# A recurrent network of two groups, one phase apart: the encoder's pass cut in two, its second layer in another PSUM bank, and five small operations moved

## The chip, the cores and the metric

The kernel runs on one core of a Trainium2 chip. The metric is the device time of one execution in microseconds (us), as the median of three runs. Engines are named as the profile names them: PE (TensorE's matmuls), PEld (its weight loads), DVE (VectorE), ACT (ScalarE), POOL (GpSimd) and SP (SyncE, which here only starts DMAs).

## The reference

2048 sequences run through 256 steps. Each step needs the state of the step before:

```python
def step(carry, xy):
    xt, yt = xy
    st, err, gs, mem, h1, c1, h2, c2 = carry
    encoded = jnp.tanh(xt @ We + st @ Ue + be)
    new_state = jnp.tanh(jnp.einsum('bd,cds->bcs', xt, Wx) + jnp.einsum('bs,cst->bct', st, Ws) + bk)
    inp = jnp.concatenate([encoded, err[:, None]], axis=1)
    mem = jnp.concatenate([inp[:, None, :], mem[:, :-1, :]], axis=1)
    a = jax.nn.relu(mem.reshape(b, -1) @ enc_w1 + enc_b1)
    agent_in = jax.nn.relu(a @ enc_w2 + enc_b2)
    h1, c1 = _lstm_cell(agent_in, h1, c1, lstm_wih1, lstm_whh1, lstm_b1)
    h2, c2 = _lstm_cell(h1, h2, c2, lstm_wih2, lstm_whh2, lstm_b2)
    gate = jax.nn.softmax(h2 @ gate_w + gate_b, axis=1)
    theta = _clamp01(jnp.mean(jnp.abs(mem[:, :10, -1]), axis=1) * 2.5)[:, None]
    gate = gate * theta + gs * (1.0 - theta)
    st = jnp.einsum('bc,bcs->bs', gate, new_state)
    pred = _clamp01(st[:, -1])
    err = pred - yt
    return ((st, err, gate, mem, h1, c1, h2, c2), pred)
```

Eight candidate states (C = 8) of 32 numbers each are mixed by a gate of 8; the memory holds 20 entries of 25 numbers; the encoder's first layer has 64 outputs, the cells 16.

## The kernel before

The batch is cut into two groups of 1024 sequences. A *round* is one phase of the program: it takes one group one step further, so there are 512 rounds, and the two groups alternate. `phase(items)` is written once for each engine. It works on up to three items, `new`, `cur` and `old` (a group at one step, at three stages of its way), in the order in which the code stands; each engine runs its own list in that order, and semaphores (`q_...`) tie the lists together. So what an engine does next is fixed, and if it waits, everything behind waits with it.

What happens to one item, by line:

- L293 transposes the group's state into PSUM, ACT copies it out (L498), L327 multiplies it for the entry, and ACT takes the tanh (L504) and an fp16 copy (L511). POOL makes the rest of the fp16 pair (L944), which SP writes into the history.
- The encoder's first layer is summed in the PSUM bank `a_ps`: 24 history matmuls (L378), spread over PE's list as filler, and the newest entry (L389). ACT takes its relu in one pass over 512 columns (`encoder1`, L517). The second layer (`encoder2`, L400) is written over the first columns of the same bank, and ACT and DVE each take half of its relu (`agent_input`, L525 and L737).
- Cell 0: ACT lays the bias into `chain` (`bias_of_cell`, L543), PE adds the products (L417, 16 records), ACT takes the tanhs (L550, L555), DVE forms the cell's terms (L705, L711), ACT a tanh (L560), DVE the hidden state (L720). Cell 1 goes the same way (the second L417 of a round, the first L705 and L711 after it), up to L729.
- The gate: logits (L427, L434), their peak (L752) and the difference from it (L757) on DVE, the exponential on ACT (`exponentials`, L574), sum, reciprocal and product on DVE (L763, L768, L774, L781). POOL makes one minus theta (`kept_share`, L877), the kept gate (`kept_gate`, L884), the exponentials times theta (L891) and the gate in SBUF (L899). DVE makes theta (`thetas`, L687) late in its phase, behind L729.
- The mix: DVE multiplies half of the candidates by the gate (L792), POOL the other half in two instructions (L911, 128x512 each; the second one also waits for the tanh of candidates' quarter 0, the L536 behind L525). DVE sums over the candidates in four instructions (`mix_sum`, L810), of which the last two stand behind the hidden state of cell 0 (L720). Their result is the next L293's input.
- POOL also keeps the new error and the prediction (`new_error` L968, `keep_prediction` L977), behind `kept_gate`.

Ahead of the loop DVE splits the candidates' and the gate's biases into fp16 pairs (L637 to L641), then the encoder's weights (L647, L648), then the rest, and sets `s_ready` (L676). SP starts the loads of weights, all five slots of x and y, and, behind `s_ready`, the first three slices of the history's weights (L223). PE waits for `s_ready` and for the bias pairs (`s_fix`).

Of the kernel before, what the change touches and what calls it, by code (L numbers as in the profile page):

```python
# [13 lines left out]
P = 128  # L14
GROUPS = 2
# [26 lines left out]
def recurrent_kernel(nc, x_l, y_l, y, error0, gate0, w, ident_c, columns_c, out):  # L42
    ctx = ExitStack()
    with ctx:
# [6 lines left out]
        def sem(name):  # L51
# [25 lines left out]
        ones = sb("ones", [P, TILES])  # L77

# [47 lines left out]
        s_out, s_ys, s_hist0 = sem("s_out"), sem("s_ys"), sem("s_history_zero")  # L126
        s_x = [sem(f"s_x_slot{u}") for u in range(PER_TILE)]
# [4 lines left out]
        (q_trps, q_st, q_zps, q_enc, q_predps, q_err, q_eh, q_el, q_aps, q_a, q_inps, q_in,  # L132
         q_candps) = (
            sem(f"q_{n}") for n in ("trps", "st", "zps", "enc", "predps", "err", "eh", "el", "aps", "a",
# [14 lines left out]
        q_in_high = sem("q_in_high")  # L149
        q_xh, q_xl = sem("q_xh"), sem("q_xl")  # L150
        q_bias = [sem(f"q_bias{c}") for c in range(2)]
        q_hkept = sem("q_hkept")
        q_sum = [[sem(f"q_sum{hf}_{pair}") for pair in range(2)] for hf in range(HF)]
# [45 lines left out]
        def _(sp):  # L199
# [11 lines left out]
            for t in range(PER_TILE):  # L211
# [4 lines left out]


            sp.wait_ge(s_parts, 1)
            sp.dma_start(gate_bias[1:2, :], gate_bias_low[0:1, :]).then_inc(s_fix, 16)
            sp.dma_start(cand_bias[1:P:D_IN, :], cand_bias_low[0:P:D_IN, :]).then_inc(s_fix, 16)  # L220
# [6 lines left out]
            sp.wait_ge(s_ready, 1)  # L227
            history_weights(w_slot(-1), PER_TILE)
            history_weights(0, PER_TILE + 1)
            history_weights(1, PER_TILE + 2)  # L230

# [53 lines left out]
        def _(pe):  # L285
            pe.wait_ge(s_ready, 1)
            pe.wait_ge(s_fix, 16 * 2)

            def state_transpose(item, hf):
                g, n, u = item  # L290
                for pair in range(2):
                    pe.wait_ge(q_sum[hf][pair], n)
# [41 lines left out]
            def candidates_bias(item):  # L334
                g, n, u = item
                for q in CAND_ORDER:
                    pe.wait_ge(q_cand[q], n)
# [106 lines left out]
            def phase(items, extra):  # L444
# [21 lines left out]
                if cur:  # L466
                    cell_gates(cur, 0)
                    candidates_bias(cur)
                    candidates_x(cur)
                    candidates_s(cur)  # L470
# [9 lines left out]
        def _(act):  # L480
# [11 lines left out]
            act.dma_start(ys[:, :, :], y.rearrange("(n p) t -> p n t", p=P)).then_inc(s_ys, 16)  # L492
            act.wait_ge(s_ready, 1)
# [607 lines left out]
```

## Time and profile before

| | |
|---|---|
| median of 3 runs | 5336.49 us (5336.03 to 5337.18) |
| the profiled execution: its time, its span | 5342.21 us, 5340.3 us |
| granted TensorE clock of that execution | 0.998 |
| busy share of the span | PE 97%, PEld 59%, DVE 84%, ACT 79%, POOL 57% |

The span is the time from the first to the last instruction of the profiled execution. Busy shares are means over the whole span. PE's is high by nature: a matmul's record reaches to the end of its pipeline, and records overlap, so 97% leaves room for waits that no row shows as idle time.

### The profile page before, as it was taken

To read this page: it belongs to the slowest core of one execution; us is meant where nothing else is said; L and a number is where in the kernel's file an instruction comes from. 1 tells how busy PE (TensorE), PEld (TensorE's weight loads), DVE (VectorE), ACT (ScalarE), POOL (GpSimd) and SP (SyncE) were. 2 spreads that over 40 slices of the span, in tenths; PEclk is the share of its full clock that TensorE was granted. 3 is DMA by queue.
4 is the path that set the end of the run, shared out by engine and by line. 5 is a ranking of instruction groups with operands and counts; after the bars stand their busy time and mean duration, and the time that the engine had idled before them with its cause. 6 is when DMAs were issued, how large, how long until landed. Compare 5 with 4: busy or idle time off the path is not lost.

```text
span 5340.3 us, 193942 instructions
## 1 busy us (share of the span) xinstructions
PE 5165.0 (97%) x68608; PEld 3158.5 (59%) x68608; DVE 4468.2 (84%) x11824; ACT 4233.4 (79%) x10241; POOL 3060.8 (57%) x6149
## 2 busy tenths in 40 slices
PE   7999999999999999999999999999999999999998
PEld 4555555555555555555555555555555555555554
DVE  7888888888888888888888888888888888888887
ACT  6887877878888878788787788788877878777886
POOL 4555555555555555555555555555555555555555
PEclk9999999999999999999999999999999999999999
DMA  2111111111111111111111111111111111111111
GB/s 68 31 30 33 30 33 30 33 30 33 30 33 30 31 31 30 33 30 33 30 33 30 33 30 33 30 32 30 30 33 30 33 30 33 30 33 30 33 30 41
DMA packets 299271, 172.29 MB, mean 32 GB/s; under 512 B 156598, under 2 KB 263866, under 8 KB 298698
## 3 DMA queue, kind: packets, MB, share of 16 engines
q1 hardware_dynamic: 293560, 159.45, 11.9%
q8 instruction: 564, 9.24, 0.7%
q10 hardware_dynamic: 5138, 3.53, 0.2%
q14 instruction: 9, 0.07, 0.0%
HBM read 74.55 MB, written 2.10 MB: 14 GB/s over the span
## 4 chain that ended last, share of the span: by engine, by line
PE 94%; ACT 4%; issue 2%; DVE 0%; DMA 0%; POOL 0%; ACTq 0%; POOLq 0%; DVEq 0%
PE a_ps L378 27%; PE chain L417 21%; PE a_ps L389 9%; PE cand_ps L359 8%; PE cand_ps L350 6%; PE chain L327 6%; PE chain L320 4%; ACT state_t L498 4%; PE chain L293 4%; PE a_ps L400 3%; PE cand_ps L340 3%; PE chain L434 1%; PE chain L427 0%; DMA gate_bias_stage<-in_gate_b 0%; DVE enc_table L648 0%
## 5 line engine op out<-in xcount | busy, mean ns | idle before, releaser
L378 PE MATMUL a_ps<-hist,w_hist 125*64 125x512 f16 x12288 | 1816.5, 383 | 25.2 <-DMA w_hist<-enc_table 24.0
L810 DVE TENSOR_REDUCE state<-mixed 128x64 f32<-128x512 f32 x2048 | 1353.4, 682 | 34.2 <-POOL mixed L911 0.8
L911 POOL TENSOR_TENSOR mixed<-cand,gate 128x512 f32<-128x512 f32 x1024 | 1285.3, 1277 | 48.6 <-POOL gate L899 12.5
L417 PEld LDWEIGHTS chain<-cell_in,cell_w 128*64 128x64 f32 x16384 | 903.2, 136 | 488.7 <-ACT cell_in L525 248.5
L417 PE MATMUL chain<-cell_in,cell_w 128*64 128x128 f32 x16384 | 1120.5, 277 | 41.5 <-issue 1.4
L536 ACT ACTIVATE cand<-cand_ps 128x512 f32<-128x512 f32 x2048 | 1107.0, 594 | 13.3 <-issue 0.4
L378 PEld LDWEIGHTS a_ps<-hist,w_hist 125*64 125x64 f16 x12288 | 695.8, 109 | 568.8 <-issue 298.1
L933 POOL CAST x_parts<-x_sb 128x256 f16<-128x256 f32 x512 | 203.8, 398 | 953.2 <-DVE cell_in L720 938.4
L550 ACT ACTIVATE gates<-chain 128x384 f32<-128x384 f32 x1024 | 503.5, 492 | 251.2 <-PE chain L417 251.2
L705 DVE SCALAR_TENSOR_TENSOR added<-gates 128x256 f32<-128x256 f32 x1024 | 620.8, 606 | 57.2 <-ACT gates L550 3.7
L877 POOL TENSOR_TENSOR one_theta<-ones,theta 128x8 f32<-128x8 f32 x512 | 105.3, 206 | 950.0 <-DVE theta L687 950.0
L543 ACT ACTIVATE chain<-cell_bias 128x512 f32<-128x512 f32 x1024 | 611.0, 597 | 16.1
L792 DVE TENSOR_TENSOR mixed<-cand,chain 128x1024 f32<-128x1024 f32 x512 | 616.4, 1204 | 0.2 <-issue 0.2
L560 ACT ACTIVATE tanh_c<-gates 128x128 f32<-128x128 f32 x1024 | 318.8, 311 | 305.1 <-DVE gates L711 305.0
L389 PE MATMUL a_ps<-entry,w_now 100*64 100x256 f32 x4096 | 555.0, 388 | 0.0
L359 PE MATMUL cand_ps<-w_s,state_t 32*128 32x256 f32 x8192 | 529.3, 375 | 0.0
L350 PE MATMUL cand_ps<-w_x_parts,x_parts 32*128 32x256 f16 x12288 | 421.5, 268 | 0.0
L327 PE MATMUL chain<-state_t,w_ue 128*64 128x256 f32 x2048 | 334.1, 405 | 87.4 <-ACT state_t L498 87.1
L517 ACT ACTIVATE a_sb<-a_ps,columns 128x512 f32<-128x512 f32 x512 | 352.3, 688 | 69.6 <-PE a_ps L389 0.8
L359 PEld LDWEIGHTS cand_ps<-w_s,state_t 32*128 32x128 f32 x8192 | 356.5, 186 | 24.7
L938 POOL TENSOR_TENSOR x_parts<-x_sb,x_parts 128x256 f16<-128x256 f32 x512 | 344.6, 673 | 41.1
L350 PEld LDWEIGHTS cand_ps<-w_x_parts,x_parts 32*128 32x128 f16 x12288 | 315.7, 93 | 71.7
(80 smaller groups left out, 7348.5 us busy)
## 6 DMA issues: line engine op xcount, KB each, us to landing
x_sb<-in_x_l SPq DMA_DIRECT2D x260, 256.0 KB, 2.7
hist<-entry_parts SPq DMA_DIRECT2D x2048, 25.0 KB
w_hist<-enc_table SPq DMA_DIRECT2D x258, 128.0 KB, 2.4
y_rows<-in_y_l SPq DMA_DIRECT2D x260, 8.0 KB
ys<-in_y ACTq DMA_DIRECT2D x1, 2048.0 KB, 16.7
preds_out<-preds SPq DMA_DIRECT2D x1, 2048.0 KB, 7.5
cand<-in_encoder ACTq DMA_DIRECT2D x1, 640.0 KB, 3.8
cell_w<-in_cell ACTq DMA_DIRECT2D x2, 256.0 KB, 5.3
```

What stands on the lines that cost most here:

```text
L327: last = nc.tensor.matmul(chain[g][rows, Z_AT:Z_AT + COLS], w_ue[:, rows], state_t[:, g, :], start=False, stop=True, skip_group_check=True)
L350: nc.tensor.matmul(cand_ps[q][:, NS * hf:NS * hf + NS], x_parts[rows, g, xp, P * hf:P * hf + P], w_x_parts[rows, wp, :], start=False, stop ...
L359: last = nc.tensor.matmul(cand_ps[q][:, NS * hf:NS * hf + NS], state_t[rows, g, P * hf:P * hf + P], w_s[rows, :], start=False, stop=True, ...
L378: nc.tensor.matmul(a_ps[g][ENC * half:ENC * half + ENC, :], w_hist[0:HROWS, w_slot(u), kk, wp, :], hist[0:HROWS, xp, k, at:at + 512], star ...
L389: last = nc.tensor.matmul(a_ps[g][rows, COLS * p:COLS * p + COLS], w_now[0:ER, p, rows], entry[0:ER, g, :], start=False, stop=True, skip_g ...
L417: last = nc.tensor.matmul(chain[g][rows, P * r:P * r + P], cell_w[c][:, hf, r, :], cell_in[c][:, g, hf, :], start=False, stop=True, skip_g ...
L536: ins = nc.scalar.activation(cand[:, g, q // 2, :, q % 2, :, :].rearrange("p h s c -> p h (s c)"), cand_ps[q][:, :].rearrange("p (h k) -> ...
L543: nc.scalar.activation(chain[g][:, :].rearrange("p (r b) -> p r b", r=4), cell_bias[:, c, :].rearrange("p (r o) -> p r o", o=1).to_broadca ...
L705: V.scalar_tensor_tensor(added[c][:, g, :, :], gates[c][:, g, 1:3, :], 1.0, gates[c][:, g, 3:5, :], ALU.add, ALU.mult).then_inc(q_added[c], 1)
L792: V.tensor_tensor(mixed[:, 1, :, :, :, :].rearrange("p h l s c -> p (h l) s c"), cand[:, g, 1, :, :, :, :].rearrange("p h l s c -> p (h l) ...
L810: V.tensor_reduce(state[:, g, hf, 2 * pair:2 * pair + 2, :], mixed[:, pair, hf, :, :, :], AX, ALU.add)\
L911: G.tensor_tensor(mixed[:, 0, :, q, :, :], cand[:, g, 0, :, q, :, :], over_s, ALU.mult)\
```

## The change

In the loop: ACT's relu of the first layer becomes two instructions of 256 columns, each with its own semaphore, and the two halves of the second layer's matmuls wait for one each. The second layer's output moves from `a_ps` to `cand_ps[2]`. Cell 0's bias is laid ahead of the exponential instead of behind `encoder1`. DVE's theta moves from behind L729 to ahead of cell 1's terms. The last two sums over the candidates become one instruction. POOL keeps error and prediction ahead of one minus theta instead of behind the kept gate. Ahead of the loop: the bias pairs are made behind `s_ready`, PE waits for them at their first use, the history's weights are fetched as soon as their table is there, four slots of x and y behind them, and ACT runs one tanh of eight columns early.

```diff
@@ (ahead of the loop: SP)
+            load_slot(0)
+            sp.wait_ge(s_tables, 1)
             history_weights(w_slot(-1), PER_TILE)
             history_weights(0, PER_TILE + 1)
             history_weights(1, PER_TILE + 2)
+            for t in range(1, PER_TILE):
+                load_slot(t)
+            sp.wait_ge(s_parts, 1)
...
@@ (PE)
             pe.wait_ge(s_ready, 1)
-            pe.wait_ge(s_fix, 16 * 2)
...
+            def candidates_bias(item, extra):
+                g, n, u = item
+                if extra is None:
+                    pe.wait_ge(s_fix, 16 * 2)
...
             def encoder2(item):
                 g, n, u = item
-                pe.wait_ge(q_a, n)
                 for p in range(2):
+                    pe.wait_ge(q_a[p], n)
                     for hf in range(HF):
                         at = AGENT_ROWS[hf].start + 2 * H * p
-                        last = nc.tensor.matmul(a_ps[g][at:at + 2 * H, 0:P], w_enc2[:, :],
+                        last = nc.tensor.matmul(cand_ps[2][at:at + 2 * H, 0:P], w_enc2[:, :],
...
@@ (ACT)
+            act.wait_ge(s_warm, 1)
+            nc.scalar.activation(warm[:, 1, :], warm[:, 0, :], ACT.Tanh)
             act.wait_ge(s_ready, 1)
...
-                nc.scalar.activation(a_sb[:, g, :], a_ps[g][:, :], ACT.Relu, bias=enc1_bias[:, 0:1])\
-                    .then_inc(q_a, 1)
+                for p in range(2):
+                    at = slice(COLS * p, COLS * p + COLS)
+                    nc.scalar.activation(a_sb[:, g, at], a_ps[g][:, at], ACT.Relu, bias=enc1_bias[:, 0:1])\
+                        .then_inc(q_a[p], 1)
...
-                nc.scalar.activation(cell_in[0][rows, g, hf, :], a_ps[g][rows, 0:P], ACT.Relu,
+                nc.scalar.activation(cell_in[0][rows, g, hf, :], cand_ps[2][rows, 0:P], ACT.Relu,
...
                     entry_high(new)
+                    bias_of_cell(new, 0)
                 if cur:
                     exponentials(cur)
                 if new:
                     encoder1(new)
-                    bias_of_cell(new, 0)
                     agent_input(new, 0)
...
@@ (DVE)
+            def last_sums(item):
+                g, n, u = item
+                dve.wait_ge(q_mul[1], n + GROUPS)
+                for q in range(2):
+                    dve.wait_ge(q_mulpool[q], n + GROUPS)
+                V.tensor_reduce(state[:, g, 1, :, :].rearrange("p (a l) s -> p a (l s)", a=2),
+                                mixed[:, :, 1, :, :, :].rearrange("p a l s c -> p a (l s) c"), AX, ALU.add)\
+                    .then_inc(q_sum[1][0], 1)
...
-                    mix_sum(old, 1, 0)
-                    mix_sum(old, 1, 1)
+                    last_sums(old)
                 if cur:
                     error_sum(cur)
                 if old:
                     prediction(old)
                 if cur:
+                    thetas(cur)
                     cell_terms(cur, 1)
...
                     second_hidden(cur)
-                    thetas(cur)
                     peaks(cur)
...
@@ (POOL)
                     next_hidden(old, cur)
+                    new_error(old, extra)
+                    keep_prediction(old, extra)
                 if cur:
                     kept_share(cur)
                     kept_gate(cur)
-                if old:
-                    new_error(old, extra)
-                    keep_prediction(old, extra)
```

How the instructions stand now shows at two places. On ACT, between the entry's fp16 copy and the tanh of candidates' quarter 0, first before and then now (each row: line, operation, output and inputs, shape, the semaphores it waits for; the changed kernel's lines are numbered some ten higher):

```order
L511 ACTIVATE entry_parts<-entry 100x256 [waits q_enc,q_err]
L574 ACTIVATE expd<-logit 128x64 [waits q_logit]
L517 ACTIVATE a_sb<-a_ps,columns 128x512 [waits q_aps]
L543 ACTIVATE chain<-cell_bias 128x512 [waits q_enc]
L525 ACTIVATE cell_in<-a_ps,columns 64x128 [waits q_inps,q_hnext]
L536 ACTIVATE cand<-cand_ps 128x2x256 [waits q_mulpool0]
```

```order
L519 ACTIVATE entry_parts<-entry 100x256 [waits q_enc,q_err]
L553 ACTIVATE chain<-cell_bias 128x512 [waits q_enc]
L584 ACTIVATE expd<-logit 128x64 [waits q_logit]
L527 ACTIVATE a_sb<-a_ps,columns 128x256 [waits q_aps]
L527 ACTIVATE a_sb<-a_ps,columns 128x256
L535 ACTIVATE cell_in<-cand_ps,columns 64x128 [waits q_inps,q_hnext]
```

The 512-column bias write has moved from behind the relu to ahead of the exponential, and the relu is two instructions, of which the second has no wait of its own. On POOL, between the copy of the hidden states and the gate, before and now:

```order
L921 COPY cell_in<-cell_in 128x256 [waits q_h0,q_hkept,s_ready]
L877 TENSOR_TENSOR one_theta<-ones,theta 128x8 [waits q_theta]
L884 TENSOR_TENSOR kept<-gate,one_theta 128x64 [waits q_keptfrom,q_onetheta]
L968 ISA [waits q_errsum,q_pred]
L968 TENSOR_TENSOR err_ring<-pred_now,ys 128x8
L977 REGISTER_ALU [waits q_pred]
L977 COPY preds<-pred_now 128x8
L944 TENSOR_TENSOR entry_parts<-entry,entry_parts 128x256 [waits q_eh]
L891 TENSOR_TENSOR weighted<-expd,theta 128x64 [waits q_exp]
```

```order
L939 COPY cell_in<-cell_in 128x256 [waits q_h0,q_hkept,s_ready]
L986 ISA [waits q_errsum,q_pred]
L986 TENSOR_TENSOR err_ring<-pred_now,ys 128x8
L995 REGISTER_ALU [waits q_pred]
L995 COPY preds<-pred_now 128x8
L895 TENSOR_TENSOR one_theta<-ones,theta 128x8 [waits q_theta]
L902 TENSOR_TENSOR kept<-gate,one_theta 128x64 [waits q_keptfrom,q_onetheta]
L962 TENSOR_TENSOR entry_parts<-entry,entry_parts 128x256 [waits q_eh]
L909 TENSOR_TENSOR weighted<-expd,theta 128x64 [waits q_exp]
```

The two instructions that wait for the prediction now stand ahead of the two that wait for theta; all four stand ahead of the entry's low half, as before.

## Rows read from the trace of the kernel before

**Rows 1.** Line view of the state's transpose: records, first and last start in us.

```profile
L293 PE MATMUL chain<-ident,state x1024: 272/300/412, 28.8 to 5308.3; 128*128 128x128 f32 x171
```

**Rows 2.** Timeline of one round, PE: start us, us, engine, line, operation, count.

```profile
2694.84 0.44 PE L293 MATMUL chain<-ident,state 128*128 128x128 f32 x2
...
2699.96 1.09 PE L417 MATMUL chain<-cell_in,cell_w 128*64 128x128 f32 x16
...
2703.28 0.60 PE L320 MATMUL chain<-x_sb,w_we 128*64 128x256 f32 x4
2703.93 1.09 PE L417 MATMUL chain<-cell_in,cell_w 128*64 128x128 f32 x16
...
2705.17 0.44 PE L293 MATMUL chain<-ident,state 128*128 128x128 f32 x2
```

**Rows 3.** Timeline of the same round, DVE.

```profile
2695.25 0.42 DVE L705 SCALAR_TENSOR_TENSOR added<-gates 128x256 f32<-128x256 f32 x1
...
2696.55 0.29 DVE L729 SCALAR_TENSOR_TENSOR h_second<-gates,tanh_c 128x128 f32<-128x128 f32 x1
...
2701.62 0.80 DVE L705 SCALAR_TENSOR_TENSOR added<-gates 128x256 f32<-128x256 f32 x1
...
2703.86 1.28 DVE L810 TENSOR_REDUCE state<-mixed 128x64 f32<-128x512 f32 x2
```

**Rows 4.** Timeline of the same round, POOL (in brackets: idle us before, and releaser).

```profile
2697.01 0.20 POOL L877 TENSOR_TENSOR one_theta<-ones,theta 128x8 f32<-128x8 f32 x1 [1.89 <-DVE theta L687]
...
2697.85 0.67 POOL L944 TENSOR_TENSOR entry_parts<-entry,entry_parts 128x256 f16<-128x256 f32 x1
2698.48 0.30 POOL L891 TENSOR_TENSOR weighted<-expd,theta 128x64 f32<-128x64 f32 x1
2699.18 0.36 POOL L899 TENSOR_TENSOR gate<-fresh,kept 128x64 f32<-128x64 f32 x1 [0.41 <-DVE fresh L774]
2699.62 2.51 POOL L911 TENSOR_TENSOR mixed<-cand,gate 128x512 f32<-128x512 f32 x2
```

**Rows 5.** Timeline of the same round, ACT.

```profile
2697.01 0.42 ACT L511 ACTIVATE entry_parts<-entry 100x256 f16<-100x256 f32 x1
2697.80 0.26 ACT L574 ACTIVATE expd<-logit 128x64 f32<-128x64 f32 x1 [0.37 <-DVE logit L757]
2698.19 0.69 ACT L517 ACTIVATE a_sb<-a_ps,columns 128x512 f32<-128x512 f32 x1
2698.77 0.59 ACT L543 ACTIVATE chain<-cell_bias 128x512 f32<-128x512 f32 x1
2699.50 0.36 ACT L525 ACTIVATE cell_in<-a_ps,columns 64x128 f32<-64x128 f32 x1
2699.89 0.60 ACT L536 ACTIVATE cand<-cand_ps 128x512 f32<-128x512 f32 x1
```

**Rows 6.** Timeline of rounds 2 and 3, PE.

```profile
38.71 0.60 PE L320 MATMUL chain<-x_sb,w_we 128*64 128x256 f32 x4
39.15 1.04 PE L417 MATMUL chain<-cell_in,cell_w 128*64 128x128 f32 x16
...
40.34 0.44 PE L293 MATMUL chain<-ident,state 128*128 128x128 f32 x2
...
50.53 0.44 PE L293 MATMUL chain<-ident,state 128*128 128x128 f32 x2
```

**Rows 7.** Timeline of round 2, POOL.

```profile
44.38 0.36 POOL L899 TENSOR_TENSOR gate<-fresh,kept 128x64 f32<-128x64 f32 x1 [0.45 <-DVE fresh L774]
```

**Rows 8.** Timeline ahead of the loop, DVE, SP's queue, PE and ACT.

```profile
5.35 2.60 DVE L637 CAST cand_bias<-cand 128x512 f16<-128x512 f32 x1 [0.79 <-DMA gate_bias_stage<-in_gate_b]
...
21.42 2.12 SPq L223 DMA_DIRECT2D w_hist<-enc_table  x3
...
24.01 3.62 PE L378 MATMUL a_ps<-hist,w_hist 125*64 125x512 f16 x16 [24.01 <-DMA w_hist<-enc_table]
...
29.45 1.28 ACT L498 ACT_TABLE_LOAD   x1 [29.45 <-PE chain L293]
```

More of the change, by code:

```diff
@@ L130, in recurrent_kernel @@
         s_hist = [sem(f"s_hist_group{g}") for g in range(GROUPS)]
[L132 removed]
+        (q_trps, q_st, q_zps, q_enc, q_predps, q_err, q_eh, q_el, q_aps, q_inps, q_in,
          q_candps) = (
[L134 removed]
+            sem(f"q_{n}") for n in ("trps", "st", "zps", "enc", "predps", "err", "eh", "el", "aps",
                                     "inps", "in", "candps"))
@@ L149, in recurrent_kernel @@
         q_in_high = sem("q_in_high")
+        q_a = [sem(f"q_a{p}") for p in range(2)]
         q_xh, q_xl = sem("q_xh"), sem("q_xl")
@@ L152, in recurrent_kernel @@
         q_hkept = sem("q_hkept")
-        q_sum = [[sem(f"q_sum{hf}_{pair}") for pair in range(2)] for hf in range(HF)]
+        q_sum = [[sem(f"q_sum0_{pair}") for pair in range(2)], [sem("q_sum1")]]
         block = ctx.enter_context(nc.Block())
@@ L210, in _, with load_slot @@
                 load(err_ring[:, :, 0:1], error0.rearrange("(n p o) -> p n o", p=P, o=1))
-            for t in range(PER_TILE):
+            def load_slot(t):
                 sp.dma_start(x_sb[:, t, :, :].rearrange("p g b -> p (g b)"), x_l[P * t:P * t + P, :])\
@@ L230, in _ @@
             history_weights(1, PER_TILE + 2)
+            for t in range(1, PER_TILE):
+                load_slot(t)
+            sp.wait_ge(s_parts, 1)
+            sp.dma_start(gate_bias[1:2, :], gate_bias_low[0:1, :]).then_inc(s_fix, 16)
+            sp.dma_start(cand_bias[1:P:D_IN, :], cand_bias_low[0:P:D_IN, :]).then_inc(s_fix, 16)
+            sp.wait_ge(s_ready, 1)
             def turn_start(turn):
@@ L286, in _ @@
             pe.wait_ge(s_ready, 1)
-            pe.wait_ge(s_fix, 16 * 2)
             def state_transpose(item, hf):
                 g, n, u = item
-                for pair in range(2):
-                    pe.wait_ge(q_sum[hf][pair], n)
+                for done in q_sum[hf]:
+                    pe.wait_ge(done, n)
                 last = nc.tensor.matmul(chain[g][:, P * hf:P * hf + P],
@@ L622, in _ @@
                 V.memset(gates[n][:, :, 4, :], 0.0)
-            for hf in range(HF):
-                for pair in range(2):
-                    V.memset(state[:, :, hf, 2 * pair:2 * pair + 2, :], 0.0).then_inc(q_sum[hf][pair], GROUPS)
+            for pair in range(2):
+                V.memset(state[:, :, 0, 2 * pair:2 * pair + 2, :], 0.0).then_inc(q_sum[0][pair], GROUPS)
+            V.memset(state[:, :, 1, :, :], 0.0).then_inc(q_sum[1][0], GROUPS)
             V.memset(scratch[:, :, :], 0.0).then_inc(s_prep, 1)
             dve.wait_ge(s_prep, 1)
-            dve.wait_ge(s_biases, 16 * 2)
             steps = [1]
@@ L676, in _ @@
             V.tensor_copy(scratch[:, 1, :], ones[:, :]).then_inc(s_ready, 1)
+            dve.wait_ge(s_biases, 16 * 2)
+            link(V.tensor_copy(cand_bias[:, :], bk_stage))
+            link(V.tensor_tensor(cand_bias_low[:, :], bk_stage, cand_bias[:, :], ALU.subtract))
+            link(V.tensor_copy(gate_bias[0:1, :], gate_bias_stage[0:1, :]))
+            V.tensor_tensor(gate_bias_low[0:1, :], gate_bias_stage[0:1, :], gate_bias[0:1, :], ALU.subtract)\
+                .then_inc(s_parts, 1)
             def error_sum(item):
@@ L736, in agent_input @@
                 dve.wait_ge(q_inps, n)
-                V.tensor_scalar(cell_in[0][rows, g, hf, :], a_ps[g][rows, 0:P], enc2_bias[rows, 0:1], 0.0,
+                V.tensor_scalar(cell_in[0][rows, g, hf, :], cand_ps[2][rows, 0:P], enc2_bias[rows, 0:1], 0.0,
                                 ALU.add, ALU.max).then_inc(q_in_high, 1)
@@ L815, in prediction @@
                 for hf in range(HF):
-                    for pair in range(2):
-                        dve.wait_ge(q_sum[hf][pair], n + GROUPS)
+                    for done in q_sum[hf]:
+                        dve.wait_ge(done, n + GROUPS)
                 V.tensor_scalar(pred_now[:, g, :].rearrange("p (h q) -> p h q", h=HF), state[:, g, :, :, S - 1],
```

16 lines of the change are left out of this document (5 added, 11 removed).

## The prediction

> **What bounds it now.** The page comes first, and its 97% for PE says little, since matmul records overlap. The line view of L293, the first instruction that a round's state needs, gives the unit of account: 1024 records in 512 rounds, from 28.8 to 5308.3 us, so (5308.3 - 28.8) / 511 = 10.33 us a round [rows 1]. Whatever the change does 512 times is counted per round; the rest of the span is some 29 us ahead and 32 us behind. Then I read the timeline of one round of that length engine by engine, all times taken from its L293 at 2694.84.
>
> PE: cell 0's products (L417) start at 5.12, the x part of the entry (L320) at 8.44, cell 1's L417 at 9.09, the next L293 at 10.33 [rows 2]. Where nothing stops PE, in round 1, L417 follows L320 by 0.44 and L293 follows L417 by 1.19 [rows 6]; here it is 0.65 and 1.24. So PE waits about 0.2 us ahead of cell 1, though no row calls it idle.
>
> What it waits for is cell 0's hidden state, done when DVE goes on to the last two sums, at 9.02. Backwards on DVE stands cell 0's L705, which took 0.80, while the same instruction for cell 1 took 0.42 [rows 3]. It ends at 7.58, 0.29 behind POOL's two L911, which ran from 4.78 to 7.29 [rows 4]: DVE's instruction had started at 6.78, but got through only when POOL let go. Backwards on POOL: L911 follows the gate (4.34), the gate the weighted exponentials (3.64), and those start only as L944 (3.01 to 3.68) ends, though the exponential was there at 3.22 [rows 4, 5]. L944 is late because four small instructions stand ahead of it that begin when theta arrives, at 2.17, after 1.89 us of idle time. Theta stands behind L729 on DVE. So the round is one loop: cell 1, theta, POOL's queue, L911, cell 0's L705, hidden state, cell 1.
>
> Round 2 tests this: it had no old error to keep, POOL reached the gate at 44.38 - 40.34 = 4.04, 0.30 sooner than above, and the round lasted 10.19 [rows 6, 7].
>
> **The change, part by part.** *Theta, and error and prediction on POOL.* The four small instructions run as soon as the prediction is out, in time in which POOL idles, so L944 starts when ACT's fp16 copy is there (2.59 and a handover) instead of at 3.01; the weighted product then waits for the exponential. *Bias ahead of the exponential.* It starts when the copy ends at 2.59, less 0.11 by which two ACT instructions overlap (L543 starts 0.11 before L517 ends), and lasts 0.59, to 3.07; the exponential can start at 2.96 as now or 0.02 later [rows 5]. Bounds 0 and 0.11 (no overlap); 0.02 taken. Together they bring the gate and the first L911 about 0.3 forward, as in round 2, to 4.5. The second L911 also needs candidates' quarter 0, whose tanh (5.05 to 5.65 now) follows `agent_input` on ACT. By the next paragraph it ends at 5.79; with some 0.1 of handover the second L911 (half of 2.51) runs from 5.88 to 7.14, L705 ends 0.29 later at 7.43 instead of 7.58, and cell 1's L417 could start 1.51 behind it, as now: at 8.94.
>
> *The relu in halves.* The same kind of instruction (relu with a bias column) takes 0.69 for 512 columns and 0.36 for 128, so about 0.47 for 256 [rows 5]. With the overlap of 0.11 the second half ends 0.36 + 0.47 = 0.83 after the start, where the whole pass ended after 0.69: **0.14 later**. The start does not move, since all halves wait for the last L389. The first half of L400 can go early, but PE is still busy with history matmuls then, and `agent_input` waits for the second half. Bounds of the delay: 0 (no column can be out sooner) and 0.25 (no overlap: 0.94 - 0.69; L536 behind L525 starts 0.03 after its end, so such pairs exist). `agent_input` and cell 0's L417 move by the same 0.14: from 5.12 to 5.26.
>
> The Trainium skill speaks against this part ("ScalarE: Activation LUTs", section What ACT_TABLE_LOAD costs: about 280 ns fixed for an instruction with a bias operand, 0.833 ns a column, 93 ns of overlap). By that page, as an estimate, a half takes 0.49 and the second ends 0.20 later than the whole pass, and the round below would be 0.06 longer. The trace gives 0.69 for 512 columns where the page gives 0.71.
>
> *The second layer's bank.* Same matmuls, same size of reads; `cand_ps[2]` is free between the error's subtraction and the candidates' bias. 0, with no gain or loss in sight: the two banks' users of before and now stand in the same order.
>
> *One sum for two.* Now 1.28 for both; one start-up less, so between 0 and 0.1 saved. They end at 10.30, just ahead of L293, and with DVE's 0.15 of gain at about 10.1. PE comes later than that (below), so this is worth nothing now.
>
> **The sum for a round.** PE's list becomes the limit: L417 of cell 0 at 5.26; L320 behind it by 3.32 as now, 8.58; L417 of cell 1 behind L320 by 0.44, at 9.02, later than the 8.94 that DVE allows; L293 1.19 later, at 10.21. Two things can still lengthen it. Cell 1's chain starts nearer to the next round's L293 now, and L434 leaves little room behind L729; and POOL's four small instructions now run while DVE makes cell 1's terms (L705 from 0.41, L729 to 2.00), where POOL was idle. I take 0.04 for both (bounds 0 and 0.3, see the rivals; near the lower end because these instructions take 0.2 to 0.3 us each, not 2.51). That makes 10.25, 0.08 less than 10.33: 511 x 0.08 = **41 us**.
>
> **Ahead of the loop.** PE's first matmul waited from 21.42 to 24.01 for weights fetched behind `s_ready`: 2.6 go, since the table is now fetched earlier. The load of ACT's table, 1.28 on the first state's way, goes too. The bias pairs leave DVE's way to `s_ready`: L637 took 2.60 [rows 8], but the next instruction may be held by what held it; bounds 0 and 2.6, 1.3 taken. Sum **5 us**. What is moved behind `s_ready` has until round 1's candidates, some 10 us later.
>
> Total 46 us: the profiled execution, 5342.21 us with a span of 5340.3, would take 5296, and the median, which is 5.7 us below that execution, **5290**.
>
> **Rivals.** *No gain in the rounds.* The halves do not overlap: 0.25 instead of 0.14, and the round is 10.21 + 0.11 = 10.32, or 10.36 with the 0.04. With the 5 us ahead of the loop that is 5336 - 5 - 5 to 5336 - 5 + 15: 5326 to 5346. For it: the pair L525 and L536. Against: L517 and L543, which like the halves cover all partitions.
>
> *Slower: POOL's small instructions hold DVE.* What L911 did to cell 0's L705, the four small instructions (about 0.9 us in a row, from the prediction on) do to cell 1's L705 and what follows it. If DVE gets through only where POOL pauses, cell 1's terms come about 0.3 later; L729, L434, L389 and the relu follow directly, and the round is 10.21 + 0.3 = 10.51: + 0.18 x 511 = 92, less 5, so 5424. It decides from about 0.12 of delay on. For it: the 0.80 against 0.42. Against: the instructions are short, and a held instruction of DVE ends only 0.29 behind the one that held it, so it could pass between two of them. No row shows DVE waiting at the border of two POOL instructions.
>
> The Trainium skill has the rule ("SBUF — State Buffer", section Who interferes with whom: a DVE instruction with two SBUF inputs and a GpSimd instruction that reads SBUF exclude each other, and the one that issues first holds the ports for all of its length). The held L705 agrees (0.80 against 0.42). By that rule DVE would get its turn at each border, which is the lesser delay.
>
> *Faster.* The halves cost nothing, or POOL's small instructions don't meet DVE: L417 of cell 0 at 5.12, cell 1's at 8.88, the round 10.07 at best, 5198; half way to it, 5245.
>
> **Chances.** The forecast (round of 10.20 to 10.29): 0.56. No gain: 0.13. Held by POOL: 0.23. More gain: 0.08. About 0.2% (11 us) is what a measurement of this kernel can tell from no change. Faster by more: 0.64; within: 0.13; slower: 0.23. The forecast's own range is 5265 to 5315; to leave out no more than 2 in 10 it goes up into the case of the held DVE, to 5365, and down to 5258.
>
> **What would show it.** Right: two relu records of about 0.47 us, the second ending 0.83 behind the first's start; weighted exponentials right behind the exponential, cell 0's L705 ending by 7.45; L417 of cell 1 following L320 by 0.44; rounds of 10.25; the first L293 some 4 us earlier, and no table load behind it. Wrong: cell 1's L705 or L711 longer than now, and L434 waiting for L729 (the slower rival); the second relu starting at the first's end (no gain); cell 1's L417 still waiting for the hidden state (POOL's queue remained the limit).

## The result, and the profile after

The changed kernel took 5268.01 us (median of 4 runs, 5267.09 to 5268.63), beside 5336.77 (5336.03 to 5337.18) of the kernel before: a ratio of 0.9871, 95% interval 0.9854 to 0.9888. It is faster by 69 us; I had forecast 5290, or 46 to 47 less than before. In the profiled execution the span is 5266.3 us, and the granted clock 0.998, as before. The views below say where the 69 us are.

The line view of the state's transpose, now L297 (records, ns min/median/max, first and last start), answers to [rows 1]:

```profile
L297 PE MATMUL chain<-ident,state x1024: 272/300/381, 24.8 to 5232.6; 128*128 128x128 f32 x171
```

A round is now (5232.6 - 24.8) / 511 = 10.19 us instead of 10.33: 511 x 0.14 = 72 us. The loop begins at 24.8 instead of 28.8, 4 us sooner. What lies behind the last transpose is 33.7 us (5266.3 - 5232.6) instead of 32.0; over the kernels of this study that tail lies between 32.0 and 37.6, so a difference of 2 us there says nothing about the change.

The timeline of one round, PE (start us, us, engine, line, operation, count), answers to [rows 2]; times in the text are taken from its L297 at 2695.04:

```profile
2695.04 0.44 PE L297 MATMUL chain<-ident,state 128*128 128x128 f32 x2
...
2700.26 1.09 PE L423 MATMUL chain<-cell_in,cell_w 128*64 128x128 f32 x16
...
2703.58 0.60 PE L324 MATMUL chain<-x_sb,w_we 128*64 128x256 f32 x4
...
2704.02 1.06 PE L423 MATMUL chain<-cell_in,cell_w 128*64 128x128 f32 x16
...
2705.23 0.44 PE L297 MATMUL chain<-ident,state 128*128 128x128 f32 x2
```

Cell 0's products start at 5.22, 0.10 later than before; cell 1's at 8.98, 0.11 sooner. Between L324 and cell 1's L423 lie 0.44 us instead of 0.65: PE no longer waits for cell 0's hidden state there. In every tenth round POOL's queue still counts: the first L929 starts at 4.68 instead of 4.52, DVE's last sum ends 0.05 later (medians), and the round lasts 10.23 (mean) instead of 10.19.

POOL in the same round (in brackets: idle us before, and releaser) answers to [rows 4]:

```profile
2695.66 0.29 POOL L986 TENSOR_TENSOR err_ring<-pred_now,ys 128x8 f32 x1 [0.34 <-DVE pred_now L837]
...
2695.90 0.19 POOL L995 COPY preds<-pred_now 128x8 f32 x1
...
2696.05 0.29 POOL L895 TENSOR_TENSOR one_theta<-ones,theta 128x8 f32<-128x8 f32 x1
...
2696.42 0.29 POOL L902 TENSOR_TENSOR kept<-gate,one_theta 128x64 f32<-128x64 f32 x1
...
2697.71 0.67 POOL L962 TENSOR_TENSOR entry_parts<-entry,entry_parts 128x256 f16<-128x256 f32 x1 [0.99 <-ACT entry_parts L519]
...
2698.37 0.29 POOL L909 TENSOR_TENSOR weighted<-expd,theta 128x64 f32<-128x64 f32 x1
...
2699.12 0.36 POOL L917 TENSOR_TENSOR gate<-fresh,kept 128x64 f32<-128x64 f32 x1 [0.45 <-DVE fresh L784]
...
2699.56 2.63 POOL L929 TENSOR_TENSOR mixed<-cand,gate 128x512 f32<-128x512 f32 x2
```

The four small instructions are done at 1.67, where the first of them used to start at 2.17. POOL then idles for 0.99 us until ACT's fp16 copy is there, and the entry's low half starts at 2.67 instead of 3.01. The gate follows at 4.08 (4.34), the two L929 end at 7.15 (7.29). The row of the two L929 is longer than before (2.63 against 2.51), since the second waits for a tanh on ACT (L546 below, done at 5.74).

ACT in the same round, answering to [rows 5]:

```profile
2697.21 0.42 ACT L519 ACTIVATE entry_parts<-entry 100x256 f16<-100x256 f32 x1
...
2697.53 0.58 ACT L553 ACTIVATE chain<-cell_bias 128x512 f32<-128x512 f32 x1
...
2698.05 0.24 ACT L584 ACTIVATE expd<-logit 128x64 f32<-128x64 f32 x1
...
2698.39 0.84 ACT L527 ACTIVATE a_sb<-a_ps,columns 128x256 f32<-128x256 f32 x2
...
2699.80 0.36 ACT L535 ACTIVATE cell_in<-cand_ps,columns 64x128 f32<-64x128 f32 x1 [0.57 <-PE cand_ps L406]
...
2700.18 0.60 ACT L546 ACTIVATE cand<-cand_ps 128x512 f32<-128x512 f32 x1
```

The relu in two halves takes 0.84 where one pass took 0.69, and `agent_input` (L535) starts at 4.76 instead of 4.66. That is where cell 0's 0.10 comes from. The exponential starts at 3.01 instead of 2.96.

DVE, answering to [rows 3]:

```profile
2695.45 0.43 DVE L715 SCALAR_TENSOR_TENSOR added<-gates 128x256 f32<-128x256 f32 x1
...
2695.98 0.29 DVE L721 SCALAR_TENSOR_TENSOR gates<-added 128x128 f32<-128x128 f32 x1
...
2696.76 0.29 DVE L739 SCALAR_TENSOR_TENSOR h_second<-gates,tanh_c 128x128 f32<-128x128 f32 x1
...
2701.92 0.55 DVE L715 SCALAR_TENSOR_TENSOR added<-gates 128x256 f32<-128x256 f32 x1
...
2703.92 1.22 DVE L828 TENSOR_REDUCE state<-mixed 128x128 f32<-128x1024 f32 x1
```

Cell 0's L715 is still held by POOL's L929 (0.55, where cell 1's takes 0.43), but ends at 7.43 instead of 7.58. Cell 1's L715 and L721 take what they took before, beside POOL's small instructions. The one last sum (L828) takes 1.22 where the two took 1.28.

Ahead of the loop, answering to [rows 8]: the timeline of POOL, DVE, ACT and PE.

```profile
0.74 6.92 POOL L888 MEMSET hist<- 128x8192 f32 x1 [0.29 <-POOLq L1088]
...
4.66 3.68 DVE L650 CAST enc_table<-cand 128x1280 f16<-128x1280 f32 x1
...
9.90 0.83 DVE L650 CAST enc_table<-cand 128x1280 f16<-128x1280 f32 x1
...
10.07 1.28 ACT L500 ACT_TABLE_LOAD   x1 [10.07 <-issue]
...
19.99 3.62 PE L384 MATMUL a_ps<-hist,w_hist 125*64 125x512 f16 x16 [19.99 <-DVE scratch L679]
```

PE starts 4.0 us sooner and now waits for DVE instead of a DMA. ACT's table is loaded long before its first use. The first L650 is slow because POOL's memset of the history (L888, to 7.66) holds it: it ended at 8.34 or 8.35 in all nine kernels with this edit, though it started anywhere from 4.66 to 4.98. In the two without it, L637 ended at 7.95 and 7.94, 0.28 behind the same memset, from starts at 5.35 and 5.81. No run moved the memset.

### The profile page after: what moved, and what is told of

Its sections match the earlier page's. It is cut to its first block, busy times and chain, and to the rows that moved or that the text cites. A ratio compares the mean times of both kernels' runs of the same rounds, so it can differ in the third digit from the quotient of the medians.

```text
span 5266.3 us, 192919 instructions
## 1 busy us (share of the span) xinstructions
PE 5127.9 (97%) x68608; PEld 3212.5 (61%) x68608; DVE 4347.6 (83%) x11313; ACT 4309.1 (82%) x10754; POOL 3224.3 (61%) x6149
## 4 chain that ended last, share of the span: by engine, by line
PE 94%; ACT 4%; issue 1%; DVE 0%; POOL 0%; POOLq 0%; DVEq 0%; ACTq 0%
PE a_ps L384 28%; PE chain L423 19%; PE a_ps L395 9%; PE cand_ps L365 8%; PE cand_ps L356 6%; PE chain L331 6%; PE cand_ps L406 5%; PE chain L324 4%; ACT state_t L506 4%; PE chain L297 4%; PE cand_ps L346 3%; PE chain L440 1%; PE chain L433 0%; DVE enc_table L650 0%; DVE enc_table L651 0%
## 5 line engine op out<-in xcount | busy, mean ns | idle before, releaser
L929 POOL TENSOR_TENSOR mixed<-cand,gate 128x512 f32<-128x512 f32 x1024 | 1301.9, 1274 | 82.2 <-POOL gate L917 12.5
L546 ACT ACTIVATE cand<-cand_ps 128x512 f32<-128x512 f32 x2048 | 1112.5, 598 | 81.1 <-issue 0.3
L423 PEld LDWEIGHTS chain<-cell_in,cell_w 128*64 128x64 f32 x16384 | 903.3, 136 | 357.4 <-ACT cell_in L535 237.8
L423 PE MATMUL chain<-cell_in,cell_w 128*64 128x128 f32 x16384 | 1105.0, 276 | 7.2 <-issue 0.8
L820 DVE TENSOR_REDUCE state<-mixed 128x64 f32<-128x512 f32 x1024 | 698.9, 682 | 18.6 <-POOL mixed L929 0.8
L962 POOL TENSOR_TENSOR entry_parts<-entry,entry_parts 128x256 f16<-128x256 f32 x512 | 343.9, 672 | 528.8 <-ACT entry_parts L519 528.8
L828 DVE TENSOR_REDUCE state<-mixed 128x128 f32<-128x1024 f32 x512 | 624.7, 1220 | 16.7 <-issue 0.9
L395 PE MATMUL a_ps<-entry,w_now 100*64 100x256 f32 x4096 | 555.3, 388 | 0.0
L715 DVE SCALAR_TENSOR_TENSOR added<-gates 128x256 f32<-128x256 f32 x1024 | 501.1, 489 | 21.4 <-ACT gates L560 4.0
L527 ACT ACTIVATE a_sb<-a_ps,columns 128x256 f32<-128x256 f32 x1024 | 429.1, 470 | 47.6 <-PE a_ps L395 0.3
L535 ACT ACTIVATE cell_in<-cand_ps,columns 64x128 f32<-64x128 f32 x512 | 185.4, 362 | 293.1 <-PE cand_ps L406 293.1
L747 DVE TENSOR_SCALAR cell_in<-cand_ps,columns 64x128 f32<-64x128 f32 x512 | 175.4, 343 | 259.5 <-PE cand_ps L406 259.5
```

The costliest lines, as they stand in the source:

```text
L395: last = nc.tensor.matmul(a_ps[g][rows, COLS * p:COLS * p + COLS], w_now[0:ER, p, rows], entry[0:ER, g, :], start=False, stop=True, skip_g ...
L423: last = nc.tensor.matmul(chain[g][rows, P * r:P * r + P], cell_w[c][:, hf, r, :], cell_in[c][:, g, hf, :], start=False, stop=True, skip_g ...
L546: ins = nc.scalar.activation(cand[:, g, q // 2, :, q % 2, :, :].rearrange("p h s c -> p h (s c)"), cand_ps[q][:, :].rearrange("p (h k) -> ...
L820: V.tensor_reduce(state[:, g, hf, 2 * pair:2 * pair + 2, :], mixed[:, pair, hf, :, :, :], AX, ALU.add)\
L828: V.tensor_reduce(state[:, g, 1, :, :].rearrange("p (a l) s -> p a (l s)", a=2), mixed[:, :, 1, :, :, :].rearrange("p a l s c -> p a (l s) ...
L929: G.tensor_tensor(mixed[:, 0, :, q, :, :], cand[:, g, 0, :, q, :, :], over_s, ALU.mult)\
```

## The experiments

The theory after the result: the round was a loop through POOL's queue; theta and POOL's order took it apart; what limits now is PE's list, behind a relu that its halves made 0.10 us later. The rivals: the halves, their bank, the bias's place or the head brought the gain. The first four kernels undo or keep one part each.

**The relu in one pass again** (all other edits stay; both halves of the second layer's matmuls wait for the one semaphore, which the cut does not show; lines are two lower from the relu on):

```diff
-                for p in range(2):
-                    at = slice(COLS * p, COLS * p + COLS)
-                    nc.scalar.activation(a_sb[:, g, at], a_ps[g][:, at], ACT.Relu, bias=enc1_bias[:, 0:1])\
-                        .then_inc(q_a[p], 1)
+                nc.scalar.activation(a_sb[:, g, :], a_ps[g][:, :], ACT.Relu, bias=enc1_bias[:, 0:1])\
+                    .then_inc(q_a[0], 1)
```

> The changed kernel with the relu of the first layer in one pass of 512 columns again; the second layer keeps its bank cand_ps[2], all other edits stay. My theory: the gain came from theta and POOL's order, the halves only cost 0.10 us a round (the second half ends 0.84 us behind the start of the first, the whole pass 0.69), and PE's list is the limit, so all of it comes back: cell 0's L423 at 5.11 instead of 5.21, rounds of 10.09 instead of 10.19, 511 x 0.10 = 51 us less than the changed kernel: 5217 us (5207 to 5235). Rival one: the second layer's first matmuls, which may start behind half one, are part of the gain: then the time rises above 5268, by up to 51. Rival two: DVE's hidden state, not PE's list, sets the round: then the delay of agent_input is hidden and the time stays within 10 us of 5268.

5222.87 us (5221.38 to 5223.34), ratio 0.9785 (0.9768 to 0.9801): 45 us less than the changed kernel. Its timeline of one round, ACT and PE:

```profile
2702.86 0.44 PE L297 MATMUL chain<-ident,state 128*128 128x128 f32 x2
...
2706.21 0.69 ACT L525 ACTIVATE a_sb<-a_ps,columns 128x512 f32<-128x512 f32 x1
...
2707.52 0.36 ACT L533 ACTIVATE cell_in<-cand_ps,columns 64x128 f32<-64x128 f32 x1 [0.62 <-PE cand_ps L406]
...
2707.98 1.09 PE L423 MATMUL chain<-cell_in,cell_w 128*64 128x128 f32 x16
...
2711.30 0.60 PE L324 MATMUL chain<-x_sb,w_we 128*64 128x256 f32 x4
...
2711.74 1.06 PE L423 MATMUL chain<-cell_in,cell_w 128*64 128x128 f32 x16
...
2712.95 0.44 PE L297 MATMUL chain<-ident,state 128*128 128x128 f32 x2
```

`agent_input` at 4.66, cell 0 at 5.12, cell 1 at 8.88, the next transpose at 10.09: the whole list moved by 0.10. So the halves are the one part of the change that costs, and they cost because PE's list is now the limit. The mean round is (5188.6 - 24.8) / 511 = 10.105, not 10.09, since one round in ten lasts some 10.24 in this kernel, hardly other than the 10.23 that it lasted in the changed one: there POOL's queue still sets the round, not PE's list.

**Theta and POOL's order alone**, in the kernel before:

```diff
                 if cur:
+                    thetas(cur)
                     cell_terms(cur, 1)
...
                     second_hidden(cur)
-                    thetas(cur)
...
                     next_hidden(old, cur)
+                    new_error(old, extra)
+                    keep_prediction(old, extra)
...
                     kept_gate(cur)
-                if old:
-                    new_error(old, extra)
-                    keep_prediction(old, extra)
```

> The kernel before with two edits alone: theta ahead of cell 1's terms on DVE, and error and prediction ahead of one minus theta on POOL. My theory: these two carry the whole gain of the rounds; with the relu in one pass, L417 of cell 0 stays at 5.12, PE's list then gives 8.88 for cell 1 and rounds of 10.08 to 10.12 instead of 10.33: 5337 - 511 x 0.21 to 0.25 = 5209 to 5230 us, faster than the changed kernel. Rival one: the halves, their bank or the bias ahead of the exponential carry it: then the time stays within 15 us of 5337. Rival two: the last two sums in two instructions (1.28 us against 1.22) end too late for the next L293: rounds of about 10.18, 5260 us.

5224.87 us (5224.31 to 5226.96), ratio 0.9788 (0.9772 to 0.9805); rounds of (5189.5 - 28.5) / 511 = 10.10. Three small instructions moved bring 112 us, more than the whole change. The rivals fall.

No run moves theta alone, or error and prediction alone, and round 2 of the kernel before says that the latter may be enough. POOL had no error and prediction to keep there, while theta came as late as ever:

```profile
42.45 0.21 POOL L877 TENSOR_TENSOR one_theta<-ones,theta 128x8 f32<-128x8 f32 x1 [2.41 <-DVE theta L687]
...
43.01 0.67 POOL L944 TENSOR_TENSOR entry_parts<-entry,entry_parts 128x256 f16<-128x256 f32 x1
```

Even so the entry's low half started at 43.01 - 40.34 = 2.67 and the gate at 4.04 [rows 7], which are the medians of the run with theta and POOL's order, and the round lasted 10.19, as long as round 2 of that run. Which of the two moves was needed stays open.

**Everything but theta and POOL's order**, the changed kernel with the diff just shown turned round:

> The changed kernel with theta behind L729's counterpart and with POOL's order as before; halves, bank, bias, one sum and the edits ahead of the loop stay. My theory: POOL's queue is the loop again (theta, the fp16 rest of the entry, weighted exponentials, gate, products, DVE's held cell-0 terms), rounds of 10.30 to 10.35, and only the 5 us ahead of the loop remain of the gain: 5320 to 5345 us. Rival one: the other edits carry the gain: the time stays within 15 us of 5268. Rival two: they carry a part of it: something between, about 5300.

5334.66 us (5333.75 to 5337.82), ratio 0.9996 (0.9986 to 1.0006); rounds of (5299.2 - 24.8) / 511 = 10.32. Its timeline shows the old loop again:

```profile
2698.25 0.44 PE L297 MATMUL chain<-ident,state 128*128 128x128 f32 x2
...
2700.34 0.21 POOL L895 TENSOR_TENSOR one_theta<-ones,theta 128x8 f32<-128x8 f32 x1 [1.81 <-DVE theta L697]
...
2701.18 0.67 POOL L962 TENSOR_TENSOR entry_parts<-entry,entry_parts 128x256 f16<-128x256 f32 x1
...
2701.26 0.24 ACT L584 ACTIVATE expd<-logit 128x64 f32<-128x64 f32 x1
...
2701.81 0.29 POOL L909 TENSOR_TENSOR weighted<-expd,theta 128x64 f32<-128x64 f32 x1
...
2702.97 2.50 POOL L929 TENSOR_TENSOR mixed<-cand,gate 128x512 f32<-128x512 f32 x2
...
2705.13 0.62 DVE L715 SCALAR_TENSOR_TENSOR added<-gates 128x256 f32<-128x256 f32 x1
```

POOL waits 1.81 us for theta, the exponential (done at 3.25) waits for the entry's low half, the two L929 follow each other without a pause. Here the halves of the relu cost nothing: the round is no longer than before the change, though `agent_input` is as late as in the changed kernel (4.76, median). A delay off the limiting loop is free, and the same delay on it cost 45 us.

**The bias behind the relu again**, in the changed kernel:

```diff
                     entry_high(new)
-                    bias_of_cell(new, 0)
...
                     encoder1(new)
+                    bias_of_cell(new, 0)
                     agent_input(new, 0)
```

> The changed kernel with cell 0's bias behind the relu again. My theory: the exponential starts 0.05 us sooner, which nothing waits for now, and the bias write of 0.59 us runs from about 4.1 to 4.7 in ACT's wait for the second layer, which lasts to 4.76: no change beyond 0.02 us a round, 5258 to 5278 us. Rival one: the second half's end and the bias together reach past 4.76, agent_input comes up to 0.10 later: up to 5320 us. Rival two: the 0.05 us of the exponential count, since the gate's chain sets the round: 5243 us.

5268.71 us (5267.89 to 5271.84), ratio 0.987 (0.9854 to 0.9887): the same as the changed kernel, as my theory had it.

**The relu in one pass and the bias behind it**, the first and the last of these diffs together:

> The changed kernel with the relu in one pass and cell 0's bias behind it again: what is left of the change is theta, POOL's order, the one last sum and the edits ahead of the loop. My theory: with the relu whole, the gate's chain and PE's list meet, so the exponential's 0.05 us now count in part: in the run with the relu alone put back, POOL's first L927 ended at 5.80, later than the second could have started (5.74), against 5.76 in the run with theta alone. Rounds of 10.097 instead of 10.105, 4 us less: 5219 us (5214 to 5223), faster than every kernel so far. Rival: the bias's place is free here too, and the time stays at 5223 within 3 us.

5219.59 us (5218.35 to 5220.1), ratio 0.9779 (0.9766 to 0.9793); rounds of (5184.4 - 23.9) / 511 = 10.099. As expected, though the 3 us to the kernel with the relu alone are less than the intervals of the two ratios; only the mean round (10.099 and 10.105) speaks for them. Most of that lies in the tenth rounds, which last 10.19 here and 10.23 there: POOL's queue sets them, and the 0.05 of the exponential counts. Against the run with theta alone it is 5 us, the part ahead of the loop. So one sum for two and the other bank are worth nothing that shows.

**The edits ahead of the loop alone**, in the kernel before:

```diff
+            sp.wait_ge(s_tables, 1)
             history_weights(w_slot(-1), PER_TILE)
...
-            pe.wait_ge(s_fix, 16 * 2)
...
+            nc.scalar.activation(warm[:, 1, :], warm[:, 0, :], ACT.Tanh)
             act.wait_ge(s_ready, 1)
...
-            link(V.tensor_copy(cand_bias[:, :], bk_stage))
...
             V.tensor_copy(scratch[:, 1, :], ones[:, :]).then_inc(s_ready, 1)
+            dve.wait_ge(s_biases, 16 * 2)
+            link(V.tensor_copy(cand_bias[:, :], bk_stage))
...
```

> The kernel before with the edits ahead of the loop alone (history's weights fetched as soon as their table is there, bias pairs behind s_ready, one early tanh). My theory: 4.0 us at the first L293 and 1.2 us in round 1, where the table load stood: 5337 - 5 = 5332 us (5329 to 5335). Rival: the rounds that follow, which are not periodic at first, give it back, or the output's DMA at the end moves as much: 5337 within 2 us.

5332.36 us (5331.97 to 5337.16), ratio 0.9991 (0.9982 to 1.0). The size is as expected, and the trace has the first transpose at 24.8, but the interval reaches to no change.

**What limits next.** In the kernel with the relu in one pass and the bias behind it, the two history matmuls ahead of the transpose are moved behind it:

```diff
-                    history(cur, 2, 2, 3)
                     state_transpose(cur, 0)
                     state_transpose(cur, 1)
                     prediction_transpose(cur)
+                    history(cur, 2, 2, 3)
```

> The kernel of e5_best with the last two history matmuls of PE's phase (0.21 us between cell 1's products and the next state's transpose) moved behind the prediction's transpose, where PE waits 0.39 us for the copy of the state. The transpose can then start 0.21 sooner. If PE's way from cell 1's products to the next transpose sets the round, as my prediction had it, the round falls by up to 0.17 (DVE's last sum then ends last): 5219 - 87 = 5132 us, 5130 to 5180. Rival, which I hold likelier after the first runs: the loop goes from cell 1's products past the transpose, over the tanhs, DVE's L739 and the logits (2.08), which stand in PE's list ahead of the newest entry's matmuls (2.23); the transpose's chain has slack, and the time stays at 5219 within 10 us.

5194.35 us (5193.31 to 5195.67), ratio 0.9732 (0.9717 to 0.9746), the fastest kernel here. Both numbers expected were wrong: 25 us, or 0.05 a round, lie between them. The timeline of one round:

```profile
2699.38 0.29 DVE L737 SCALAR_TENSOR_TENSOR h_second<-gates,tanh_c 128x128 f32<-128x128 f32 x1
...
2699.73 0.34 PE L440 MATMUL chain<-gate_w,h_second 128*64 128x64 f32 x4
...
2699.89 1.04 PE L395 MATMUL a_ps<-entry,w_now 100*64 100x256 f32 x8
...
2706.50 1.06 PE L423 MATMUL chain<-cell_in,cell_w 128*64 128x128 f32 x16
...
2707.49 0.51 PE L297 MATMUL chain<-ident,state 128*128 128x128 f32 x2
```

The transpose follows cell 1 by 0.99 instead of 1.21. But cell 1's own way is as long as it was: tanhs, DVE's hidden state (L737, done at 2699.67), logits (L440, 0.06 behind it), and the newest entry's matmuls (L395) stand behind those in PE's list. Over all rounds the logits followed the hidden state by 0.10 (median) without the move and by 0.06 with it, and the relu followed L395's start by 1.12 and 1.10; these and differences of 0.01 are the 0.05 gained. The first of the two expectations was thus right on what limits, but another way was only 0.05 behind. That cell 1's way holds the rest is read from the trace; no run has shortened it, though the long probe below lengthens it.

**How far POOL holds DVE.** Two probes put one more instruction, whose result nothing reads, between POOL's copy of the prediction and one minus theta of the changed kernel (the call is written out in place, the tile that it writes is left out):

```diff
                     keep_prediction(old, extra)
+                    G.tensor_tensor(probe[:, :], w_x[:, :], w_x_parts[:, 0, :], ALU.subtract)
```

> The changed kernel with one more instruction on POOL, behind the prediction's copy and ahead of one minus theta: a subtraction of constants, 128x256 into fp16 like the entry's low half (0.67 us), whose result nothing reads. It tells how far POOL's work holds DVE where the change put the small instructions. The rival of the prediction (POOL holds DVE): the new instruction starts when DVE's L721 ends at 1.21, lasts to about 1.88, and holds L739, which ended at 1.98 and then ends some 0.15 to 0.25 later; PE's logits and the newest entry's matmuls behind them follow, and the round is 10.34 to 10.44: 5345 to 5396 us. The other theory (only POOL's queue matters): kept gate ends at about 2.3, still ahead of the entry's low half at 2.67, so nothing is later: 5268 us within 8. Between the two, if L739 gets through while POOL runs: 5280 to 5330.

5271.35 us (5270.27 to 5273.27), ratio 0.9877 (0.9862 to 0.9892); rounds of (5233.4 - 24.8) / 511 = 10.19. Of the 3 us more, 2 lie outside the span (5271.04 against 5267.2 in the profiled execution, where the changed kernel has 5268.21 against 5266.3). Nothing in the round is later, but the trace (first two rows below) gives no verdict on the rival: the probe ended only 0.05 behind the start of L740, which took its 0.29. So a longer one at the same place, 320 columns of fp32:

```diff
-                    G.tensor_tensor(probe[:, :], w_x[:, :], w_x_parts[:, 0, :], ALU.subtract)
+                    G.tensor_tensor(probe[:, :], cell_w[0].rearrange("p h r b -> p (h r b)")[:, 0:5 * HALF],
+                                    cell_w[1].rearrange("p h r b -> p (h r b)")[:, 0:5 * HALF], ALU.subtract)
```

> The changed kernel with one more instruction on POOL at the same place as in the probe before, but longer: a subtraction of two fp32 constants, 128x320 into fp32. The short probe was held by DVE's second cell-1 instruction until 1.21 and then took 0.53 us for 256 columns, to 1.74, 0.05 behind the start of DVE's hidden state of cell 1 (1.69, end 1.98, neither later than without it). At L929's rate (1.28 us for 512) the long one takes 0.80 from 1.21 and ends at 2.01. Theory (whoever issues first holds the other, if both read two inputs from SBUF): the hidden state, ready at 1.69, gets through only behind POOL and ends 0.29 behind it, at 2.30 instead of 1.98; the logits, and the newest entry's matmuls behind them in PE's list, follow, rounds of 10.44 to 10.50: 5396 to 5427 us. Rival (POOL holds nobody here, only its own queue counts): kept gate ends at 2.70, the entry's low half starts at about 2.65 as now, and the time stays at 5271 to 5285 us.

5293.26 us (5292.94 to 5295.13), ratio 0.9911 (0.9895 to 0.9928); rounds of (5255.9 - 24.9) / 511 = 10.24. That is 25 us more than the changed kernel, 23 of them in the rounds. The timelines of the short probe, then of the long one:

```profile
2696.57 0.76 POOL L999 TENSOR_TENSOR probe<-w_x,w_x_parts 128x256 f16<-128x256 f32 x1
...
2697.28 0.29 DVE L740 SCALAR_TENSOR_TENSOR h_second<-gates,tanh_c 128x128 f32<-128x128 f32 x1
```

```profile
2687.40 0.29 DVE L722 SCALAR_TENSOR_TENSOR gates<-added 128x128 f32<-128x128 f32 x1
...
2687.47 0.96 POOL L999 TENSOR_TENSOR probe<-cell_w 128x320 f32<-128x320 f32 x1
...
2687.73 0.42 DVE L709 TENSOR_TENSOR entry<-cand_ps,y_rows 4x256 f32<-4x256 f32 x1
...
2688.18 0.40 DVE L740 SCALAR_TENSOR_TENSOR h_second<-gates,tanh_c 128x128 f32<-128x128 f32 x1
```

L740 starts as early as before, but takes 0.40: it ends 0.15 behind the probe (2688.58 against 2688.43). So the hold exists at this place too, and POOL's own queue is not the cause, since the kept gate was done (at 2.52, median) before the entry's low half could start (2.67). The price, 23 to 25 us, was a fifth or less of the one expected, for three reasons: the probe ended at 1.94 (median), not 2.01; DVE ended 0.15 behind it, not 0.29; and of the 0.10 by which L740 came later, 0.05 a round arrived.

## Why the prediction was right, and where its sizes were off

*The loop through POOL's queue* was right, and the run with theta and POOL's order alone shows it: rounds of 10.10, where the "faster" rival had 10.07 at best for halves that cost nothing. The run without theta shows the rest.

*Theta and POOL.* The four small instructions fit where POOL idled. The forecasts of the second L911 (5.88 to 7.14) and of cell 0's L705 (7.43) were met: the two L929 end at 7.15, L715 at 7.43.

*The relu in halves* was the term that was mis-sized: 0.14 forecast, 0.10 measured at `agent_input`. The second half does end 0.15 later than the whole pass (0.84 against 0.69). But only four of L406's eight matmuls are left then, and the last of them started 0.19 behind the relu's end, where it had been 0.22 for the whole pass (medians); the handover to ACT gave back the rest. By the Trainium skill ("ScalarE: Activation LUTs", What ACT_TABLE_LOAD costs) the second half would, as an estimate, have ended 0.19 later (280 ns fixed less 93 ns of overlap), with 0.49 for a half. The 0.20 of the prediction sets the same halves against the trace's whole pass. The trace has 0.470 for a half and an overlap of 0.10, so the measurement lies below.

*PE's list as the new limit* was right: L324 0.44 ahead of cell 1's L423, which is not waiting for DVE. L423 to L297 took 1.21, not 1.19. What the prediction did not see is that cell 1's way over the logits is only 0.05 shorter, and that one round in ten stays with POOL's queue.

*The 0.04 for L434's room and the hold* was the second mis-sized term: nothing. With 0.04 less for the relu, 0.04 less here, and 0.02 more behind cell 1, 10.25 becomes the 10.19 measured. From first to last transpose it is (5308.3 - 28.8) - (5232.6 - 24.8) = 72 us less, of which 1 is the table load of round 1, which I had counted ahead of the loop: 71 us instead of 41. The median gained less than that says: the profiled execution of before, in which I counted the rounds, lay 5.7 us above its median, that of the changed kernel only 0.2, and the tail is 1.7 longer. 30 - 6 - 2 = 22 us, by which the time fell below the forecast. The round, 10.19, lies just outside the 10.20 to 10.29 that the forecast named. That the time still lies within its 5265 to 5315 is luck: without these 8 us it would have been 5260, inside the range only where that goes down to 5258. (0.04 above 10.25 gives 5310, not 5315.)

*The slower rival* (0.23) did not come. At this place it is DVE that issues first, and POOL that waits, as the line view of the new error shows:

```profile
L986 POOL TENSOR_TENSOR err_ring<-pred_now,ys x512: 212/395/402, 46.0 to 5255.3; 128x8 f32 x170, 128x8 f32<-128x8 f32 x1
```

The same instruction had a median of 218 ns before; it now ends 0.07 us behind cell 1's L715 (0.91 against 0.84, medians), and POOL has 0.99 us to spare there. The long probe shows a place from which on the rival counts: an instruction of POOL that reached 0.25 us past the start of DVE's hidden state (1.94 against 1.69, medians) cost 23 us in the rounds. By the Trainium skill ("SBUF — State Buffer", Who interferes with whom) whichever of the two issues first holds the ports for all of its length. The trace agrees in both directions: DVE ended 0.15 behind the long probe, and POOL's subtraction 0.07 behind L715. DVE's L709, which reads one of its inputs from PSUM, ran through the probe at its usual 0.42.

*The bias*: 0.05 later for the exponential, where I took 0.02 (bounds 0 and 0.11); without effect on the time beside the halves.

*Ahead of the loop*: 5 us forecast; 4.0 at the first transpose, and the first round is 1.2 shorter (10.28 against 11.50). The held instruction passed its hold on, as feared: L650 took 3.68 for what its second like took 0.83 for. The time was lost to POOL's memset, which the prediction did not name. The whole was still what I had summed.

## What to carry to other kernels

Where engines run fixed lists, look at what stands ahead of the instruction on which a round waits, however small, and at what input comes late: moving one 128x8 instruction on DVE and two on POOL was worth 112 us (no run separates the two moves), and all the other edits together lost 43 of them. Price every other edit against the limit that will hold *after* the main one: the split relu did not lengthen the old loop and cost 45 us in the new one. A change that bundles edits should be taken apart again: the fastest kernels here are the change without the cut that its title names.

## What the hardware showed unexpectedly

An instruction of DVE with two inputs from SBUF that POOL holds is recorded with its early start, and ends a while behind the holder, longer for the larger of the two seen: 0.15 us for 128x128, 0.28 for 128x256 (median; 0.29 in [rows 3, 4]). A cast with one input from SBUF did the same behind POOL's memset: 0.28 for 128x512, 0.68 for 128x1280. The same holds the other way round: POOL's 128x8 subtraction, 218 ns (median) where nothing held it, ended 0.07 us behind the DVE instruction that held it. So in such pairs the length of a record tells who waited, and its start does not tell when the work began.
